# A selective scan whose third input comes by DMA: dt*u of every third step spread over the states

## What is computed

```python
def step(h, inp):
    u_t, d_t, B_t, C_t = inp
    dA = jnp.exp(d_t[..., None] * As)
    h = h * dA + (d_t * u_t)[..., None] * B_t[:, :, None, :]
    y = jnp.einsum('bkcn,bkn->bkc', h, C_t)
    return (h, y)
h0 = jnp.zeros(u.shape[1:] + (As.shape[-1],), u.dtype)
_, ys = jax.lax.scan(step, h0, (u, d, Bt, Ct))
```

## Time and profile before

| what | us |
|---|---|
| median of 3 runs | 4128.41 (4120.87 to 4129.06) |
| the profiled execution | 4141.09 |
| its span, first to last instruction | 4139.3 |
| first scan stage, from the first scan on | 732.8 |
| second scan stage | 756.2 |

### The profile page before, as it was taken

The page is one execution under the profiler, slowest core; times in us unless marked ns, Lnnn a source line. Parts: engine busy times, 40 slices in busy tenths (PEclk is TensorE's granted clock), DMA queues, the critical chain, the costliest instruction groups (busy, mean ns, idle before and its releaser), DMA issues. The chain is left out here.

```text
span 4139.3 us, 114059 instructions
## 1 busy us (share of the span) xinstructions
PE 3704.4 (89%) x49016; PEld 1900.6 (46%) x49016; DVE 3223.0 (78%) x3434; ACT 2433.9 (59%) x4310; POOL 1570.4 (38%) x1171
## 2 busy tenths in 40 slices
PE   6788875899999977699999998959999999999998
PEld 4477742333333333233333334715655655655653
DVE  5565455799898966689988867769889888898881
ACT  2266625444444435344444443618999999999995
POOL 0132210799999930589999870010000000000000
PEclk9799987789888878678888788959999999999999
DMA  5343216222221114322122122531221212222211
GB/s 131 80 75 72 56 33 195 54 68 53 56 64 49 44 46 129 106 58 63 47 59 62 44 57 66 165 79 53 58 58 56 57 52 58 59 56 58 58 42 51
DMA packets 142716, 282.21 MB, mean 68 GB/s; under 512 B 67031, under 2 KB 93783, under 8 KB 135172
## 3 DMA queue, kind: packets, MB, share of 16 engines
q1 hardware_dynamic: 141492, 273.54, 25.1%
q10 hardware_dynamic: 720, 1.38, 0.1%
HBM read 180.62 MB, written 93.67 MB: 66 GB/s over the span
## 5 line engine op out<-in xcount | busy, mean ns | idle before, releaser
L2216 DVE TENSOR_REDUCE l3a_mx<-l3a_mx 128x2 f32<-128x768 f32 x1296 | 1165.1, 951 | 161.5 <-PE l3a_mx L2115 157.4
L2182 ACT ACTIVATE l3a_p<-l3a_s 128x384 f32<-128x384 f32 x2592 | 1180.4, 492 | 114.9 <-PE l3a_s L2129 106.5
L1438 POOL TENSOR_TENSOR l_scan_sc<-l_scan_s,l_scan_repc 128x768 f32<-128x768 f32 x576 | 1031.8, 1809 | 136.8 <-PE l_scan_y L1329 102.2
L1380 ACT ACTIVATE l_scan_da<-l_scan_da,l_k_a 128x768 f32<-128x768 f32 x576 | 503.9, 875 | 777.5 <-PE l_scan_da L1302 777.4
L2129 PE MATMUL l3a_s<-l3a_q,l3a_k 125*32 125x384 f16 x10368 | 805.1, 327 | 5.4 <-DMA l3a_q<-l3a_m 3.6
L1302 PE MATMUL l_scan_dup<-l_scan_dtu,l_k_pick 32*128 32x384 f32 x2304 | 662.0, 650 | 102.9 <-DMA l_scan_dtu<-l_dtp 46.4
L2115 PE MATMUL l3a_mx<-l3a_k,l3a_q 124*32 124x384 f16 x10368 | 673.7, 335 | 58.9 <-DMA l3a_q<-l_qx 31.6
L1302 PE MATMUL l_scan_da<-l_scan_dtu,l_k_pick 32*128 32x384 f32 x2304 | 653.1, 649 | 28.4 <-DVE l_scan_s L1416 23.0
L2141 PE MATMUL l3a_o<-l3a_p,l3a_vh 128*32 128x288 f32 x6912 | 569.9, 405 | 0.4 <-ACT l3a_p L2182 0.4
L2083 POOL TENSOR_TENSOR l3a_norm<-l3a_out,l3a_spread 128x576 f32<-128x576 f32 x24 | 34.5, 1436 | 1343.6 <-DMA l3a_spread<-l_inverses 1343.6
L1396 DVE TENSOR_TENSOR l_scan_bu<-l_scan_dup,l_scan_repb 128x768 f32<-128x768 f32 x384 | 362.7, 944 | 153.7 <-PE l_scan_dup L1302 113.1
(11 more groups left out here) (192 smaller groups left out, 3723.5 us busy)
## 6 DMA issues: line engine op xcount, KB each, us to landing
l3a_q<-l_qx SPq DMA_DIRECT2D x96, 486.0 KB
l_scan_repb<-l_bcp SPq DMA_DIRECT2D x48, 384.0 KB
l_scan_repc<-l_bcp SPq DMA_DIRECT2D x46, 384.0 KB
l_dtp<-l_prep_t SPq DMA_DIRECT2D x16, 864.0 KB, 7.3
l_dup<-l_prep_d SPq DMA_DIRECT2D x16, 864.0 KB, 7.4
l_scan_dtu<-l_dup SPq DMA_DIRECT2D x96, 144.0 KB
l_scan_dtu<-l_dtp SPq DMA_DIRECT2D x92, 144.0 KB
l_y<-l_o_ys SPq DMA_DIRECT2D x24, 288.0 KB
```

Source lines behind the costliest of these rows:

```text
L1380: act.activation(da_ps[st % 2][:, MID], da_ps[st % 2][:, MID], ACT.Exp, scale=A[:, column:column + 1]).then_inc(exped, 1)
L1438: pool.tensor_tensor(SC[:, st % NSC, :], S[:, n, :], REPC[k % 2][:], ALU.mult).then_inc(weighted, 1)
L2182: act.activation(P[:, k % NP, third * SW:(third + 1) * SW], s_ps[u % NS_PS][:, 0:SW], ACT.Exp)\
L2216: dve.tensor_reduce(MX[:, qt % (NB * KT), 2 * pair:2 * pair + 2], mx_ps[n % NR][:, :, 0:RG], AX_X, ALU.max)\
```

## The change

dt*u of each triple's third step no longer goes through PE, PSUM and ACT. SP fetches it from DRAM with a broadcast source, each of its 8 rows repeated for 16 states, straight into one of NP = 4 buffers BUP; POOL multiplies it there in place. PE restores dt*u for steps 0 and 1 of a triple only, one ahead, and none in the third step; it waits on DVE's `multiplied` alone. ACT's copy and DUS are gone. A spread waits for the scan that used its buffer four triples before. Spreads 0 to 3 are issued at the start, around the load of chunk 1; those of later triples at the head of SP's part for each chunk, before `load_chunk(k + 2)`.

```diff
+    NP = 4
...
-        DUS = s.sb("dus", [128, 2, TC])
-        BUP = s.sb("bup", [128, 2, TC])
+        BUP = s.sb("bup", [128, NP, TC])
...
+        spread = [s.sem(f"spread{i}") for i in range(NP)]
...
-        order = [GP]
-        for st in range(STEPS):
-            nxt = st if st % NT != GP else st + NT
-            if nxt < STEPS:
-                order.append(nxt)
+        order = [st for st in range(STEPS) if st % NT != GP]
...
+                def spread_du(tr):
+
+                    k, p, d, c, n = place(tr * NT + GP)
+                    first = (n % NT) * 32 + n // NT * 8
+                    if tr >= NP:
+                        sp.wait_ge(scanned, (tr - NP) * NT + GP + 1)
+                    sp.dma_start(BUP[:, tr % NP, :], du_dram[p, first:first + 8, span(c)].unsqueeze(1)
+                                 .to_broadcast([8, NS, TC])).then_inc(spread[tr % NP], 16)
...
                 load_first()
+                spread_du(0)
+                spread_du(1)
                 load_chunk(1)
+                for tr in range(2, NP):
+                    spread_du(tr)
                 for k in range(CHUNKS):
+                    for tr in range(k * NG + NP - 1, (k + 1) * NG + NP - 1):
+                        if NP <= tr < TRIPLES:
+                            spread_du(tr)
                     if k + 2 < CHUNKS:
                         load_chunk(k + 2)
...
                     if m >= 1:
-                        before = order[m - 1]
-                        if before % NT == GP:
-                            pe.wait_ge(du_copied, before // NT + 1)
-                        else:
-                            pe.wait_ge(multiplied, dve_steps_before(before) + 1)
+                        pe.wait_ge(multiplied, m)
                     restore(st, 64, du_ps, du_made)
...
-                for st in order[0:2]:
-                    restore_du(st)
+                restore_du(0)
                 for st in range(STEPS + LAG):
                     if st < STEPS:
                         if st >= 2:
                             pe.wait_ge(scanned, st - 1)
+                        if st % NN == 0:
+                            pe.wait_ge(loaded[st // NN % 2], (st // NN // 2 + 1) * 64)
                         restore(st, 0, da_ps[st % 2], dt_made)
-                    if st + 2 < len(order):
-                        restore_du(order[st + 2])
+                    if st % NT != GP and nth_du.get(st, len(order)) + 1 < len(order):
+                        restore_du(order[nth_du[st] + 1])
...
-                    if st % NT == GP and st + NT < STEPS:
-                        copy_du(st + NT)
...
-                    pool.wait_ge(du_copied, tr + 1)
-                    if tr >= 2:
-                        pool.wait_ge(scanned, (tr - 2) * NT + GP + 1)
-                    pool.tensor_tensor(BUP[:, tr % 2, :], DUS[:, tr % 2, :], REPB[k % 2][:], ALU.mult)\
+                    pool.wait_ge(spread[tr % NP], 16 * (tr // NP + 1))
+                    pool.tensor_tensor(BUP[:, tr % NP, :], BUP[:, tr % NP, :], REPB[k % 2][:], ALU.mult)\
                         .then_inc(pool_multiplied, 1)
```

More of the change, by code:

```diff
@@ L1199, in ssm_scan @@
         rep_loaded = [s.sem(f"rep_loaded{i}") for i in range(2)]
-        du_made, dt_made, exped, multiplied, du_copied, pool_multiplied = (
-            s.sem(n) for n in ("du_made", "dt_made", "exped", "multiplied", "du_copied", "pool_multiplied"))
+        du_made, dt_made, exped, multiplied, pool_multiplied = (
+            s.sem(n) for n in ("du_made", "dt_made", "exped", "multiplied", "pool_multiplied"))
+        spread = [s.sem(f"spread{i}") for i in range(NP)]
         scanned, weighted, piece_summed, y_taken = (
             s.sem(n) for n in ("scanned", "weighted", "piece_summed", "y_taken"))
-        order = [GP]
-        for st in range(STEPS):
-            nxt = st if st % NT != GP else st + NT
-            if nxt < STEPS:
-                order.append(nxt)
+        order = [st for st in range(STEPS) if st % NT != GP]
         nth_du = {st: n for n, st in enumerate(order)}
@@ L1253, in load_chunk @@
                     if k >= 2:
-                        last = (k - 1) * NN
-                        sp.wait_ge(dt_made, last)
-                        sp.wait_ge(du_made, nth_du[last - 1] + 1)
+                        sp.wait_ge(dt_made, (k - 1) * NN)
+                        sp.wait_ge(du_made, (k - 1) * NG * (NT - 1))
                     for row, src in ((64, du_dram), (0, dt_dram)):
@@ L1364, in take_y @@
                     act.activation(home, y_ps[:, 0:TC], ACT.Copy).then_inc(y_taken, 1)
-                def copy_du(st):
-                    tr = st // NT
-                    act.wait_ge(du_made, nth_du[st] + 1)
-                    if tr >= 2:
-                        act.wait_ge(pool_multiplied, tr - 1)
-                    act.activation(DUS[:, tr % 2, :], du_ps[:, MID], ACT.Copy).then_inc(du_copied, 1)
-                copy_du(GP)
                 for st in range(STEPS):
                     k, p, d, c, n = place(st)
-                    if st % NT == GP and st + NT < STEPS:
-                        copy_du(st + NT)
                     column = p % 4 * NN + n
@@ L1404, in _ @@
                         dve.wait_ge(pool_multiplied, st // NT + 1)
-                        bu = BUP[:, st // NT % 2, :]
+                        bu = BUP[:, st // NT % NP, :]
                     else:
```

## The result

The changed kernel takes 4018.7 us (median of 4 runs, 4013.4 to 4029.8), the kernel before 4128.7 beside it: a ratio of 0.9726, with a 95% interval from 0.9679 to 0.9774. That is 110 us less where 52 were forecast. The way was right, the size twice what the likeliest case said, and close to the second rival, in which the clock stays up.

What follows compares the result with a forecast made beforehand. VectorE, with GpSimd nearly as full, bounds the scan stages at TensorE's 2.4 GHz, TensorE at 1.2. Stage gains of 27 and 29 us, less 2 x 2 at the start, give 52: 4141 - 52 - 12.7 = 4076 us, range 4015 to 4150.

Steps and rivals of the forecast that it cites:

- likeliest case: Whole kernel: 52 us less, 4076 us, within 4040 to 4100; chance 0.45.
- second rival: Scan stages: TensorE's clock stays up, all at GpSimd's pace, 4002 us, or 4034 with 0.15 slow; chance 0.17.
- The sum leaves the work done at each level as it was: Scan stages: chunks run at each clock level stay 17.8 and 6.2 in the first, 15.2 and 9.0 in the second.
- prices of 28.0 and 33.5 us: Time of a chunk after the change: 28.0 us at TensorE's 2.4 GHz, 33.5 us at 1.2 GHz.
- first and third rivals: First: TensorE stays slow, 4186 us at 0.8 slow, chance 0.13. Third: late spread becomes the wait, 4138 us, chance 0.08.
- VectorE's 1.5 us at chunk ends: Triple after each chunk's end, 2.4 GHz: VectorE's 1.50 us wait before its multiply can go, a chunk on VectorE 27.3 us.
- The third restore: TensorE's dt*u restore in the GpSimd step: nothing at 2.4 GHz; at 1.2 GHz 0.54 us less a triple, 8.37.
- GpSimd's lag is absorbed between 27.3 and 28.4 us a chunk: Chunk at 2.4 GHz: 27.3 us if GpSimd's lag is always absorbed, 28.4 if never; 28.0 taken.
- The spreads cost nothing: 96 spread loads a stage: DMA share from 0.20 to 0.40, no price on compute engines, 2 us at each stage's start.
- The late spread: Chunk's last triple, backward passes: spread issued behind the store of y, landing after 5.6 us; just fits, nothing in the sum.
- The first rival, thinner work: Scan stages: less TensorE work a round makes its clock fall inside chunks; 4186 us at 0.8 slow; chance 0.13.
- ACT's copy is hidden except at the chunk's end: ACT's dt*u copy, 0.80 us, 96 times a stage: hidden under TensorE except at chunk ends, where 1.50 us can go.

Runs made afterwards that it cites:

- e9: Kernel before, with three unused 128 x 128 matmuls by TensorE at each chunk's end ahead of its restore of dt, order otherwise kept: 4029.4 us, ratio 0.9751.
- e4: Changed kernel, with ACT making a second, unused copy of y at each chunk's end: 4031.7 us, ratio 0.9761.
- e5: Kernel before, with only ACT's take of y moved one exponential later, all work kept: 4022.0 us, ratio 0.9735.
- e2: Changed kernel with all dt*u restores back in the order of the kernel before, ACT's copy still gone: 4015.0 us, ratio 0.9722.
- e10: Changed kernel with all dt*u restores back, no ACT copy, and every 16th triple's third product made by VectorE from PSUM: 4028.4 us, ratio 0.9757.
- e1: Changed kernel with the restores, ACT's copy and the waits of the kernel before put back, so only the spreads are added: 4145.0 us, ratio 1.0031.
- e12: Changed kernel with three unused filling matmuls by TensorE at each chunk's end: 4056.7 us, ratio 0.9812.
- e7: Changed kernel, with every 8th or 16th triple's product by B made by VectorE in SBUF instead of GpSimd: 4112.3 us (8th), 4101.3 us (16th).

## Why the prediction was wrong in size

The step that failed is the one that the prediction called its weakest: "The sum leaves the work done at each level as it was". It kept 220 and 318 us a stage at 1.2 GHz; the changed kernel has 0.17 of 676 us there, some 117 each. With that share and the prediction's own prices of 28.0 and 33.5 us a chunk is 28.8, and the stages gain 105 us: 56 were forecast for them and 138 measured. So the share is some 50 of the 82 us that were missing. The other 32 lie in the prices and in how they were added, see below. The text had the mechanism, "the change closes most of this gap, which speaks for fewer falls", and set beside it the thinner work, with 0.17 for a clock that stays up. What the trace of before could have told is that nearly all falls sat at the chunk's end, 32 of 33, just where the change closes a gap from 0.86 to 0.17 us. That this is the cause is shown for the kernel before (e9); e4 and e5, which have gaps of 0.75 and 1.55 us there and 3 and 12 falls behind them, show that the gap's length alone doesn't tell how many falls there will be, and what does stays open. The second rival, all at GpSimd's pace, gave 4002 to 4034 us, and 4018.7 lies in the middle of it. In part that is luck: its sign, a clock over 0.92, was just missed with 0.91, and at the measured share its own formula gives 4039.

The sums hold when they are worked again, but for the chances: the first and third rivals come to 0.21, not 0.19.

Point by point:

- *VectorE's 1.5 us at chunk ends goes.* Right: 8.1 to 8.2 us became 6.9. But as time it was worth little in itself, 7 to 15 us a stage and not 36 (24 x 1.5) (e9), since GpSimd's 28.4 us a chunk stood right under the 28.6. The prediction saw this cap and took 28.0 for a fast chunk.
- *The third restore.* 8.37 us a triple was forecast at 1.2 GHz, 8.11 measured: the round without it is 2.59, as said, and one of the other two 2.60 in place of 2.89. Of this the restore is the smaller part: with it and without the copy (e2, e10) a slow triple takes 8.43, so 0.3 us are the restore's and 0.5 come from the copy or TensorE's wait for it, which the prediction held to be hidden there. The restore's worth in time is nil (e2): TensorE was the bound only in the slow stretches, and GpSimd's pace now covers these.
- *GpSimd's lag is absorbed between 27.3 and 28.4 us a chunk.* In part: a stage is 675.8/24 = 28.2 us a chunk, slow stretches included. In the sum, fast and slow chunks were added each at its own price. The trace shows VectorE at 6.86 us a triple while fast, ahead of GpSimd's 7.1, and at 8.1 while slow, where it loses that lead. Its own mean comes out at GpSimd's pace, so the stage is the larger of the two, not the sum of the parts.
- *The spreads cost nothing*, share 0.40: right, 0.41, and e1 bears it out. The first scan of the stage starts 3 us later in the profile; VectorE's wait for the first loads is 42.8 us over both stages, 3.6 more than before, 1.8 a stage where 2 were taken.
- *The late spread.* Right that it is issued behind the store of y, and that it just fits; GpSimd's lag of one triple makes it harmless. VectorE waits for no GpSimd product longer than 1.2 us.
- *The first rival, thinner work.* It doesn't show: with all restores (e2) there are 18 falls, without them 16. These lie in ten different steps of the chunk, none in step 7 and 2 in step 8, so most are of another kind than those of before. Only their length speaks for the rival, since the slow share is 17% to e2's 12 and 13.
- *ACT's copy is hidden except at the chunk's end.* Right at 2.4 GHz, and more than was made of it: had the prediction asked what moving the take of y alone would do, it would have found the 110 us without the change.

## What to carry to other kernels

Before taking work away from TensorE, look at where its clock falls: if the falls share one place in the loop, find what the engines wait for just before it and ask what stands in front of that instruction. Here an in-order queue (ACT: y, then the copy, then the exponential) made TensorE wait 0.86 us and VectorE 1.50 once in 28 us; moving two lines, or filling TensorE's gap, gave as much as the whole change. Count the falls afterwards, for the gap's length didn't foretell them. And when several engines are within a few per cent of one another, price a stage as the largest of their sums over fast and slow stretches together, since a saving on one of them is hidden until the others have moved too.

## What the runs showed of the hardware

- Three unused matmuls in a gap of TensorE's, 0.94 us once a chunk, took the falls of its clock from 33 to 1 and 100 us off the kernel (e9). The same three where there was no gap made 16 falls into 24 and cost 38 us (e12). A gap of 1.55 us at 43 of 48 chunk ends was followed by a fall 12 times (e5), one of 0.75 at 40 was so 3 times (e4). The Trainium skill ("TensorE: Matmul & The Clock Gate", Part 1: The HAM clock gate) says that activity lifts the slow level and idleness brings it back; the first pair of runs agrees as to the direction, though here the clock fell after TensorE had been busy 2.14 of 3.00 us and not idle throughout. The second pair shows that more matmuls alone don't lift it; where its later falls come from stays open.
- A VectorE multiply of two float32 tiles in SBUF, 128 x 768, took up to 8.2 us while GpSimd worked back to back (e7), and 0.94 with one of them in PSUM (e10). The Trainium skill ("GPSIMD Engine Reference", section 1, Specifications) says that VectorE instructions with two SBUF inputs contend with GpSimd for its SBUF interfaces; the trace agrees, and gives the size: with every 16th triple ten of twelve waited until GpSimd's row of instructions had ended, with every 8th the median was 2.1 us.
- A restore of dt and one of dt*u, which stand in different rows of the array, share a round of 2.60 us at 1.2 GHz when both start at once (1111.59 and 1111.60), against 2.59 for the round of dt alone: the second restore is free there. Where it starts 0.34 us later the round is 2.92.
